# Attention, first head group: one head's squares moved from ScalarE to VectorE in three of five steps

## What is computed

```python
qkv = x @ qkv_w.T + qkv_b
q, k, v = (qkv[:, :, 0], qkv[:, :, 1], qkv[:, :, 2])
scores = jnp.einsum('bnhd,bmhd->bhnm', q, k) * scale
t = jnp.square(scores + C_SHIFT)
attn = t / jnp.sum(t, axis=-1, keepdims=True)
out = jnp.einsum('bhnm,bmhd->bnhd', attn, v).reshape(B, N, D)
```

## Time and profile before

| what | value |
| --- | --- |
| device time, median of 3 runs | 4254.01 us (4253.61 to 4260.93) |
| profiled execution: span from its first to its last instruction | 4333.9 us |
| profiled execution: time of its own besides the span | none is given |
| PE, busy share of the span | 84% |
| DVE, busy share | 67% |
| ACT, busy share | 53% |
| POOL, busy share | 38% |
| attention stage in the trace | about 2050 to 3720 us |
| outputs of group 0, four times | from 2221.6, 2616.9, 3015.2 and 3412.9 us |

### The profile page before, as it was taken

One profiled execution on the slowest core, in us unless ns is written; L12 is line 12 of the kernel. 1 busy time (PEld: TensorE's weight loads), 2 busy tenths in 40 slices (PEclk: granted clock), 3 DMA queues, 4 the chain that ended last, 5 costly groups with the idle time before them and its releaser, 6 DMA issues. The chain is left out here.

```text
span 4333.9 us, 64637 instructions
## 1 busy us (share of the span) xinstructions
PE 3640.3 (84%) x24130; PEld 2345.7 (54%) x24130; DVE 2902.6 (67%) x2667; ACT 2306.3 (53%) x3514; POOL 1641.7 (38%) x734
## 2 busy tenths in 40 slices
PE   5779899898889989997688978888988889288787
PEld 1257777777777777776334342434333342256565
DVE  6258888888888888887767574767566673643311
ACT  1376667666667766663354637454654645342221
POOL 1257877777877777886000000000000000224422
PEclk9899999999999999999799999999999999588898
DMA  5500101110101110101201110111112010424433
GB/s 198 157 32 31 40 17 41 40 36 31 41 20 38 41 36 32 40 12 58 57 1 53 43 41 12 51 52 24 23 56 57 1 24 30 140 89 146 136 114 116
DMA packets 119427, 238.94 MB, mean 55 GB/s; under 512 B 22246, under 2 KB 83982, under 8 KB 116018
## 3 DMA queue, kind: packets, MB, share of 16 engines
q1 hardware_dynamic: 107266, 203.22, 15.0%
q0 software_dynamic: 11392, 31.02, 2.2%
q10 hardware_dynamic: 432, 0.20, 0.0%
HBM read 135.85 MB, written 79.27 MB: 50 GB/s over the span
## 5 line engine op out<-in xcount | busy, mean ns | idle before, releaser
L712 DVE TENSOR_TENSOR prod<-ps,win 128x1792 f32<-128x1792 f32 x630 | 1241.4, 2018 | 159.9 <-PE ps L783 116.1
L783 PE MATMUL ps<-ident,prod 128*128 128x128 f32 x8820 | 1093.6, 280 | 168.3 <-DVE prod L712 152.9
L783 PEld LDWEIGHTS ps<-ident,prod 128*128 128x128 f32 x8820 | 1027.6, 145 | 313.0 <-DVE prod L712 170.1
L1699 POOL DMA_DIRECT2D ident<-in_ident x1 | 0.6, 578 | 1627.7 <-POOLq L925 1627.7
L1168 ACT ACTIVATE phq<-ps 128x896 f32<-128x896 f32 x448 | 384.7, 918 | 201.0 <-PE ps L1431 200.1
L1266 DVE TENSOR_TENSOR phk<-kv 128x2048 f32<-128x2048 f32 (+1 forms) x200 | 455.9, 2282 | 1.2 <-issue 0.7
L468 POOL TENSOR_TENSOR y<-a1w,x2w 128x1568 f32<-128x1568 f32 x98 | 320.8, 3274 | 326.6 <-PE ps L763 308.3
L611 ACT ACTIVATE ps<-lg 128x448 f32<-128x448 f32 (+1 forms) x322 | 315.2, 982 | 239.9 <-DVE prod L712 239.9
L632 ACT ACTIVATE lg<-ps,par 128x392 f32<-128x392 f32 x392 | 390.9, 997 | 32.7 <-PE ps L770 31.3
L625 ACT ACTIVATE y<-ps,u2c,s2c 128x392 f32<-128x392 f32 x392 | 266.8, 681 | 223.9 <-PE ps L763 221.8
L762 PE MATMUL ps<-y,cw1bd 128*128 128x392 f32 x784 | 330.2, 503 | 36.2 <-ACT y L618 29.0
(11 more groups left out here) (264 smaller groups left out, 5314.3 us busy)
## 6 DMA issues: line engine op xcount, KB each, us to landing
win<-planes SPq DMA_DIRECT2D x14, 2480.0 KB, 8.7
qst<-qsp SPq DMA_DIRECT2D x96, 196.0 KB, 4.5
planes<-stage SPq DMA_DIRECT2D x7, 1984.0 KB, 7.0
xs<-in_x SPq DMA_DIRECT2D x8, 1568.0 KB, 21.3
conv_dram<-osb SPq DMA_DIRECT2D x14, 896.0 KB, 4.6
t<-in_x SPq DMA_DIRECT2D x28, 448.0 KB, 4.0
xn<-conv_dram SPq DMA_DIRECT2D x28, 448.0 KB, 6.9
t_dram<-tout SPq DMA_DIRECT2D x28, 448.0 KB, 2.9
```

The source lines that it names most:

```text
L712: v.tensor_tensor(prod[b.buf(t)][:].rearrange("p (s h w) -> p s h w", h=RW, w=W), w, xw, ALU.mult).then_inc(prod_ready, 1)
L783: mm = pe.matmul(acc[:, at:at + P], x[:, at:at + P], ident[:], start=(t == 0 and k % 4 == 0), stop=(t == NU - 1), is_transpose=True, skip_ ...
```

## The change

The second pair's square is split where `hg == 0` and the step f is 0, 2 or 3. ScalarE then squares head 2 alone (448 columns in place of 896). VectorE copies head 3's sums out of PSUM into a new tile `qh` and multiplies `qh` by itself into `phq`. `phq_done` becomes three counters: `phq_a` (ScalarE's squares), `phq_c` (VectorE's copies) and `phq_v` (VectorE's products). The selection of the second pair waits for `phq_a` and, where the step before was split, `phq_c`; the output matmuls wait for `phq_a` and, where split, `phq_v`. VectorE's order in a chunk of group 0 becomes: copy and product of step 0, product into `at` for the chunk before, reciprocal, copy and product of step 2, `weigh` for the next chunk, copy and product of step 3. The last `at` product stands behind the last chunk. Group 1 keeps its order. Two counters that nothing waits on (`qf_done`, `out_gate`) go away; the one increment of `out_gate` goes to `gate`, which nothing waits on either.

```diff
+        qh = sb("qh", [P, CT])
...
+        V_F = (0, 2, 3)
+        def by_vector(hg, f):
+            return hg == 0 and f in V_F
+        def vector_squares(b, c, f):
+            return (b * NCT + c) * len(V_F) + V_F.index(f) + 1
...
-                sp.sem_inc(out_gate, 1)
+                sp.sem_inc(gate, 1)
...
-                            src = ps[:, 2 * hp:2 * hp + 2, 0:CT]
-                            dst = phq[k % 2][:, 2 * hp:2 * hp + 2, :]
+                            top = 3 if hp == 1 and by_vector(hg, f) else 2 * hp + 2
+                            src = ps[:, 2 * hp:top, 0:CT]
+                            dst = phq[k % 2][:, 2 * hp:top, :]
                             if f < FT - 1:
-                                act.activation(dst, src, ACT.Square).then_inc(phq_done, 1)
+                                act.activation(dst, src, ACT.Square).then_inc(phq_a, 1)
...
+                def square(c, f):
+                    k, n = c * FT + f, vector_squares(b, c, f)
+                    v.wait_ge(sel_mm, b * HG * NSEL + hg * NSEL + 2 * k + 2)
+                    if k >= 1:
+                        v.wait_ge(phq_v, n - 1)
+                    v.tensor_copy(qh[:], ps[:, 3, 0:CT]).then_inc(phq_c, 1)
+                    if k >= 2:
+                        v.wait_ge(o_mm, b * HG * NCT * FT + hg * NCT * FT + k - 1)
+                    v.wait_ge(phq_c, n)
+                    v.tensor_tensor(phq[k % 2][:, 3, :], qh[:], qh[:], ALU.mult).then_inc(phq_v, 1)
...
+                    if hg == 0:
+                        square(c, 0)
+                        if c >= 1:
+                            divide(c - 1)
+                        invert(c)
+                        square(c, 2)
+                        if c + 1 < NCT:
+                            weigh(c + 1)
+                        square(c, 3)
+                        continue
...
+                if hg == 0:
+                    divide(NCT - 1)
...
-                        pe.wait_ge(phq_done, b * HG * NSEL + hg * NSEL + n - 1)
+                        pe.wait_ge(phq_a, b * HG * NSEL + hg * NSEL + n - 1)
+                        if hp == 1 and by_vector(hg, (k - 1) % FT):
+                            pe.wait_ge(phq_c, vector_squares(b, (k - 1) // FT, (k - 1) % FT))
...
-                    pe.wait_ge(phq_done, b * HG * NSEL + hg * NSEL + 2 * k + 2)
+                    pe.wait_ge(phq_a, b * HG * NSEL + hg * NSEL + 2 * k + 2)
+                    if by_vector(hg, f):
+                        pe.wait_ge(phq_v, vector_squares(b, c, f))
```

More of the change, by code:

```diff
@@ L975, in attention_stage @@
         gate = sem("gate2")
-        out_gate = sem("out_gate2")
         x_in = [sem(f"x_in2{c}") for c in range(NCT)]
@@ L982, in attention_stage @@
         q_mm = sem("q_mm")
-        qf_done = sem("qf_done")
         qh_done = sem("qh_done")
@@ L1001, in attention_stage @@
         sel_mm = sem("sel_mm")
-        phq_done = sem("phq_done")
+        phq_a = sem("phq_a")
+        phq_c = sem("phq_c")
+        phq_v = sem("phq_v")
         o_mm = sem("o_mm")
@@ L1100, in queries @@
                         act.wait_ge(qst_in, 16 * (b * HG * 3 * HPG + 3 * HPG))
-                    act.activation(at[:, hg, ch(c)], bank, ACT.Identity, bias=bq_s[:, hg:hg + 1]).then_inc(qf_done, 1)
+                    act.activation(at[:, hg, ch(c)], bank, ACT.Identity, bias=bq_s[:, hg:hg + 1])
                     act.activation(qsp[:, 0, ch(c)], bank, ACT.Identity, bias=bq_s[:, hg:hg + 1]).then_inc(qh_done, 1)
@@ L1164, in squares @@
                                 act.wait_ge(o_mm, b * HG * NCT * FT + hg * NCT * FT + k - 1)
-                            src = ps[:, 2 * hp:2 * hp + 2, 0:CT]
-                            dst = phq[k % 2][:, 2 * hp:2 * hp + 2, :]
+                            top = 3 if hp == 1 and by_vector(hg, f) else 2 * hp + 2
+                            src = ps[:, 2 * hp:top, 0:CT]
+                            dst = phq[k % 2][:, 2 * hp:top, :]
                             if f < FT - 1:
-                                act.activation(dst, src, ACT.Square).then_inc(phq_done, 1)
+                                act.activation(dst, src, ACT.Square).then_inc(phq_a, 1)
                             else:
-                                act.activation(dst, src, ACT.Square, bias=selb[:]).then_inc(phq_done, 1)
+                                act.activation(dst, src, ACT.Square, bias=selb[:]).then_inc(phq_a, 1)
                         beside = more and hg == 1 and c >= 2
@@ L1300, in weigh, with divide, invert @@
                     v.scalar_tensor_tensor(qt[c % 2][:], ps[:, 5, 0:CT], kbar[:], at[:, hg, ch(c)], ALU.add, ALU.mult).then_inc(qt_done, 1)
+                def square(c, f):
[8 more added lines that the diff above has]
+                    v.tensor_tensor(phq[k % 2][:, 3, :], qh[:], qh[:], ALU.mult).then_inc(phq_v, 1)
+                def divide(c):
+                    n = b * HG * NCT + hg * NCT + c
+                    v.wait_ge(rd_done, n + 1)
+                    v.wait_ge(qt_done, n + 1)
+                    v.wait_ge(o_mm, b * HG * NCT * FT + hg * NCT * FT + (c + 1) * FT)
+                    v.tensor_tensor(at[:, hg, ch(c)], ps[:, out_bank(hg, c), 0:CT], rd[c % 2][:], ALU.mult).then_inc(att, 1)
+                def invert(c):
+                    n = b * HG * NCT + hg * NCT + c
+                    v.wait_ge(den_done, n + 1)
+                    v.reciprocal(rd[c % 2][:], rd[c % 2][:]).then_inc(rd_done, 1)
                 v.wait_ge(gram_done, 2 * (b * HG + hg) + 2)
@@ L1304, in outputs @@
                 for c in range(NCT):
-                    n = b * HG * NCT + hg * NCT + c
                     beside = more and hg == 1 and c >= 2
+                    if hg == 0:
[8 more added lines that the diff above has]
+                        continue
                     if beside:
                         residual(b + 1, c - 2)
-                    v.wait_ge(den_done, n + 1)
-                    v.reciprocal(rd[c % 2][:], rd[c % 2][:]).then_inc(rd_done, 1)
+                    invert(c)
                     if beside:
@@ L1316, in outputs @@
                         norm.scale(v, b + 1, c - 2)
-                    if hg == 1 and c >= 1:
+                    if c >= 1:
                         join(b, c - 1)
[L1319 to L1322, removed]
+                    divide(c)
+                if hg == 0:
+                    divide(NCT - 1)
             def body(b, more):
```

## The result

| | before | after |
| --- | --- | --- |
| device time, median of 14 runs each | 4256.84 us | 4244.84 us |
| ratio of the runs | | 0.9974 (0.9966 to 0.9981) |
| span of the profiled execution | 4333.9 us | 4248.9 us |

The change gains 12.0 us by the medians, 11.1 us by the ratio (8.1 to 14.5). The forecast was 14.7 us and 4239.3 us; the measured median lies in the range.

What follows compares the result with a forecast made beforehand. TensorE plus a ring with ScalarE was taken as the bound; 0.69 us a middle chunk, 3.7 an image with first and last chunks, 14.7 in all, took 4254.0 to 4239.3 us. Own range 4234 to 4245, 8-in-10 range 4233 to 4253.

Steps and rivals of the forecast that it cites:

- TensorE's floor: TensorE's own work in one chunk of group 0's outputs, without waits: 10.42 us of the 11.47 measured.
- a ring of TensorE and ScalarE: In group 0's chunks TensorE waits for ScalarE's squares, losing 0.32, 0.39 and 0.33 us in steps 0, 1 and 3.
- parts 1 and 2: Split squares: ScalarE's one-head square 0.55 us, VectorE's copy 0.62 and product 0.62, the latter two filling idle time.
- the slower rival: VectorE's copy shares PSUM reads with ScalarE and takes 1.24 us, making the kernel slower, 4278 us; chance 0.11.
- The drain: A flush after each VectorE instruction, as added time 0.7 us a square and some 31 us in all; chance 0.02.
- Step 1's wait: TensorE's wait for ScalarE in the unsplit step 1 of group 0's chunks, said to shrink from 0.39 to about 0.35 us.
- part 3: Group 0's first chunk gains only step 3's 0.33 us; the last gives back step 0's 0.32 and 0.1 more.
- part 4: Added TensorE waits at selections and output matmuls, and changed order: cost taken as 0, bound 8.4 us.
- What is gained here is gained at the end: The next stage starts on the last `at` product, so the whole 14.7 us should reach the device time.
- VectorE's slack: Spare time before TensorE needs VectorE's copies and products in group 0's middle chunks: never under 0.25 us.
- the late rival: VectorE's split squares take 0.2 to 0.3 us more and bind the chunk; gain 7.9 to 0.8 us; chance 0.18.
- The larger gain: Step 1's wait in group 0's chunks disappears too, 8 us more gained, 4231 us; chance 0.05.

Runs made afterwards that it cites:

- steps 0 and 3 alone: The changed kernel with step 2's split taken out; 0.9951 of the time of the kernel before, 21 us less.
- step 0 alone: The changed kernel with the splits of steps 2 and 3 taken out; 0.9988 of the time of the kernel before, 5 us less.
- steps 0, 1 and 3 at 10.50: The changed kernel with step 1 split in place of step 2, chunk 10.50 us; 0.9948 and, again, 0.9953 of the time of the kernel before.
- 448 columns added: The changed kernel with an unused 448-column VectorE product between copy and product of each split square; 1.0063 of the time of the kernel before.
- in the second pair: Kernel before and changed kernel each profiled and timed once more without edit; 1.0 and 0.9972 of the time of the kernel before.

## Why the prediction was right

1. **The bound.** TensorE's floor and a ring of TensorE and ScalarE in steps 0, 1 and 3: shown. Each split takes away its own step's wait and, but for 0.04 to 0.08 us in step 1, no other (steps 0 and 3 alone, step 0 alone, steps 0, 1 and 3 at 10.50 against the floor of 10.42).
2. **Durations** (parts 1 and 2): right to 0.02 us. The shared read of PSUM, the slower rival's mechanism, is not there: the 55 copies that lie wholly beside a square of ScalarE took 0.62 us, and with 448 columns added step 3's copies, which lie mostly outside the squares, took 0.62 as well (those behind the reciprocal take 0.56). Its price was right, though: +0.65 a square made the kernel 27 us slower. The drain of the Trainium skill, VectorE: DVE Perf Modes, section "The DRAIN you can't avoid", taken as added time, did not show either: a product starts 0.59 to 0.73 after its copy starts, mostly 0.03 to 0.04 after its end, and an instruction that waits for nothing 0.54 after the product's start, as in the earlier trace rows.
3. **The middle chunk**: 10.78 forecast, 10.80 measured, so 0.68 for 0.69. Step 1's wait went to 0.31, not 0.35. In the last image a chunk went from 11.32 to 10.70, 0.62; the sum took the rows of image 1 for all four.
4. **First and last chunk** (part 3). The last chunk gives back a little more than was said: its output matmuls of step 4 start 7.91 us after those of step 0, where the prediction's figures come to 7.83. The kernel with steps 0 and 3 alone shows by which edit: 0.57 us an image from the split of step 2. The prediction had seen that step 2 loses nothing, and did not draw from it that its split only costs.
5. **Added waits** (part 4): nothing to be seen, as the middle chunk is at 10.80. Group 0's outputs gained 15.1 and 14.8 us for a sum of 14.7, and part of that agreement is luck. Of it 1.3 and 1.1 us lie in the first chunks, which vary with the place of TensorE's slow stretch. Where that lay at the same place in both kernels, the first `at` product came no sooner (20.06 us before and 20.14 after, 20.37 and 20.45, 20.62 and 20.64). Without that an estimate from these numbers is 13.5 us, 1.2 less than the sum: 0.5 in the middle chunks, the rest in the first and last ones.
6. **"What is gained here is gained at the end"** failed in part. 12.0 of the 14.7 us arrived in the medians. In the first profiles 5.0 us were lost in group 1's first chunks by where TensorE's slow stretch ended; in the second pair 0.5. As the slow stretch ends early or late in repeats of one kernel, no cost of the change is shown by it, but it blurs a gain of this size. Whether the missing 3 us are all of this kind is open: the interval of the ratio reaches to 14.5.
7. **VectorE's slack** was mis-sized: 0.08 us a square, not 0.25. The prediction did not keep to its own 0.25: its figures for the late rival (11.03 at +0.2, 11.34 at +0.3) put the bend at 0.11 to 0.12, and the 0.15 in place of 0.05 from product to output matmuls is what is missing from there to 0.08. The late rival was nearer than its 0.18: 0.1 us more on a copy, and the gain would have begun to shrink.

The larger gain (step 1's wait gone as well) did not come by itself; it takes the split of step 1.

## What to carry to other kernels

Where two engines hand one buffer to and fro, subtract the bound engine's floor from each step and split only the steps that wait: here one of three splits was worth nothing, and moving it to the step that waited was worth another 7 to 8 us in the outputs, though not all of it could be seen in the device time. A slack that several instructions of one chain share has to be divided by their number. And look at what the bound engine does after a long idle gap: filling two gaps an image with idle matmuls was worth 15 to 16 us, where the whole change was worth 11 to 12.

## What the runs showed of the hardware

- After gaps of 4.3 to 4.5 us TensorE's pair of 128x448 products took 1.68 to 1.86 us for 1.02 in 73 of 80 cases, with a granted clock of 0.50 for all or most of it; in the other seven the clock was back at 1.00 before the pair. That moment differed in repeats of one kernel. With the gaps filled the pair took 1.02 in all 24 cases, and the first chunks of the four images agreed to 0.09 us.
- TensorE's output matmuls start 0.15 us after the VectorE product that they wait for (80 cases in three kernels), and 0.05 after a ScalarE square that they wait for; selections start 0.05 after ScalarE's square.
- The same kernel takes 4257 us on one chip and 4342 on another, and the difference lies behind the attention stage: 659 to 669 us from the last `at` product to the end in the five profiles of the slower kind, 578 to 585 in the eight others.
